# Preparation of a transformer block in another order: three table loads, x statistics block by block, and the later rotation tables made inside later groups

## What is computed

```
x = x + layernorm(attention(layernorm(x)))
x = x + layernorm(ffn(layernorm(x)))

# attention, per head h (64 complex dimensions)
q, k, v = complex projections of x
ang = t * [omega, -omega];  qr, kr = q*exp(i ang), k*exp(i ang)      # rotation tables: sin and cos of ang
E = exp(clip(-mu_h * |t - t'|, -30, 0))
s = Re(qr . conj(kr));  maha = max(|q|^2 + E^2 |k|^2 - 2 E s, 0) / V
logits = coef * log1p(maha / nu) - 32 * log(V);  A = causal softmax(logits);  y = A v
```

## Time and profile before

| what | us |
|---|---|
| runs | 1907.39, 1908.41, 1909.68 |
| median | 1908.41 |
| the profiled execution | 1907.7 |
| its span in the trace | 1905.9 |

### The profile page before, as it was taken

How to read it: one execution, slowest core, us unless ns; L and a number is a source line. 1 busy time by engine, 2 the same in 40 slices (tenths; PEclk the granted TensorE clock), 3 DMA queues, 4 the chain that set the end, 5 groups by cost and what they waited for, 6 DMA issues and landing times.

```text
span 1905.9 us, 40909 instructions
## 1 busy us (share of the span) xinstructions
PE 1798.5 (94%) x10672; PEld 1477.9 (78%) x10672; DVE 1609.2 (84%) x3842; ACT 1578.6 (83%) x3224; POOL 1453.4 (76%) x1288
## 2 busy tenths in 40 slices
PE   4589999999999999999999999999999999998997
PEld 3377788887888887887888778887888788876876
DVE  7788898888888887888888878888888888996884
ACT  5779888898888887888888888888888888886664
POOL 5367788888888887888888877888888888872663
PEclk8799999999999999999999999999999999999998
DMA  7313101231122111311013111211131111010111
GB/s 210 119 40 111 62 24 44 78 94 45 45 78 88 33 42 47 110 62 46 33 69 94 46 47 64 89 43 46 45 111 45 46 45 42 26 54 14 45 45 45
DMA packets 61087, 117.72 MB, mean 62 GB/s; under 512 B 13488, under 2 KB 42928, under 8 KB 52704
## 3 DMA queue, kind: packets, MB, share of 16 engines
q1 hardware_dynamic: 59936, 115.51, 18.0%
q10 hardware_dynamic: 960, 0.00, 0.0%
HBM read 99.64 MB, written 21.36 MB: 63 GB/s over the span
## 4 chain that ended last, share of the span: by engine, by line
PE 60%; DVE 10%; POOL 8%; issue 6%; ACT 2%; DVEq 0%; POOLq 0%; ACTq 0%
PE pa L786 13%; PE ps L826 11%; PE py L850 10%; PE po L861 9%; PE pp L816 7%; PE pp L838 5%; POOL qk L608 4%; PE pa L797 3%; PE pa L805 2%; DVE lg L1607 2%; DVE stats L1645 1%; POOL ek L618 1%; DVE ps L1596 1%; DVE lg L1615 1%; DVE acc L1667 1%
## 5 line engine op out<-in xcount | busy, mean ns | idle before, releaser
L608 POOL TENSOR_TENSOR qk<-rm 64x512 f32<-64x512 f32 x504 | 684.2, 1357 | 102.7 <-PE ps L826 44.2
L618 POOL TENSOR_TENSOR ek<-tabs,kn 128x512 f32<-128x512 f32 (+3 forms) x512 | 460.7, 906 | 151.7 <-DVE lg L1607 112.1
L1615 DVE CUSTOM_DVE_ANT_0 lg<-lg,tabs,ncog 128x512 f32<-128x512 f32 (+3 forms) x512 | 442.6, 883 | 0.6 <-issue 0.6
L786 PE MATMUL pa<-xt,wt 128*128 128x512 f32 x1488 | 424.4, 421 | 12.5 <-issue 6.9
L826 PE MATMUL ps<-qk 128*128 128x512 f32 (+3 forms) x1024 | 375.0, 450 | 25.0 <-DVE lg L1607 24.9
L1488 DVE TENSOR_TENSOR rm<-pa,tabs 128x512 f32<-128x512 f32 x504 | 327.9, 678 | 70.8 <-POOL qk L608 65.7
L1607 DVE CUSTOM_DVE_ANT_0 lg<-ps,ek,qb 128x512 f32<-128x512 f32 (+3 forms) x512 | 279.5, 546 | 125.3 <-POOL ek L618 82.7
L850 PE MATMUL py<-pt,vt 128*128 128x128 f32 x2560 | 347.9, 275 | 0.1
L850 PEld LDWEIGHTS py<-pt,vt 128*128 128x128 f32 x2560 | 330.6, 191 | 16.5 <-issue 0.3
L786 PEld LDWEIGHTS pa<-xt,wt 128*128 128x128 f32 x1488 | 275.9, 193 | 66.1 <-issue 11.2
L1186 ACT ACTIVATE lg<-lg,qb 128x512 f32<-128x512 f32 (+3 forms) x512 | 278.5, 558 | 19.4 <-DVE lg L1607 15.9
(11 more groups left out here) (193 smaller groups left out, 2245.2 us busy)
## 6 DMA issues: line engine op xcount, KB each, us to landing
xt<-xs_d SPq DMA_DIRECT2D x56, 1024.0 KB, 4.8
tabs<-vec_d SPq DMA_DIRECT2D x7, 1536.0 KB, 9.6
xs_d<-xt SPq DMA_DIRECT2D x6, 1024.0 KB, 4.0
wt<-wraw_d SPq DMA_DIRECT2D x7, 768.0 KB, 5.6
acc<-in_L_attn_x SPq DMA_DIRECT2D x8, 512.0 KB, 6.0
tabs<-in_L_attn_x SPq DMA_DIRECT2D x8, 512.0 KB, 4.9
out<-tabs SPq DMA_DIRECT2D x8, 512.0 KB, 3.1
tabs<-rope_d SPq DMA_DIRECT2D x56, 64.0 KB, 4.1
```

Of the source, the lines that this page charges most:

```text
L608: pool.tensor_tensor(qk[part * DH:(part + 1) * DH, z * HH + hh, :], rm[row, 2 * part, :], rm[row, 2 * part + 1, :], ALU.add if part else A ...
L618: pool.tensor_tensor(ek[:, n % 2, 0:w], tab(par, hh, E2_T, w), kn[:, hh, 0:w], ALU.mult).then_inc(ek_pool, 1)
L786: last = mm(pa[r][:, :], wproj(par, z, kt, a, r * P, (r + 1) * P), xbuf[x][:, kt, b, :], start=(n == 0), stop=(n == 3 * KT - 1))
L1615: dve.tensor_tensor_reduce(lg[:, hh, at(n)], lg[:, hh, at(n)], tab(par, hh, T3_T, w), ncog[:, par, 0, hh:hh + 1], 3e38, ALU.add, ALU.min, ...
```

## The change

1. ACT: the DMA of mu and its two activations come first, the sine table is loaded once, and all logarithms lie behind it: three table loads ahead of body 0 in place of five. The four omega DMAs move from ACT's queue to SP's.
2. x statistics go block by block; blocks 4 to 7 in bodies 0 to 3, behind `decay(c, 1, 3)`; before, two blocks each in bodies 0 and 1.
3. Of the feed-forward weights only one cast, two transposing steps and two keeps stay ahead of body 0; the rest are in body 0.
4. Body 0 makes only the first part of the rotation tables, with its five DVE instructions spread over the body, and ACT then waits for their store. Parts 1 to 3 are made in the free table tile `tabs[0]` in bodies 9, 10, 11 and 25, 26, 27 and 41, 42, 43: five angle instructions and a small copy on DVE over three bodies, and four activations on ACT in the third. The inner loop of those groups is written out for that.
5. Group 1's tables are loaded in body 5 (before 2 and 3), later groups' in their body 4 (before 2 and 3).

On ACT, ahead of body 0:

```diff
-            for k in range(ROPES):
-                act.dma_start(om[:, k:k + 1], omega_d[4 * k:4 * k + 4, :].rearrange("a (d e) -> (a d) e", e=1)).then_inc(om_all, 16)
...
+            act.wait_ge(mu_in, 16)
+            a_step(act.activation(hp[:, 6:7], hp[:, 0:1], ACT.Abs))
+            a_step(act.activation(hp[:, 11:12], hp[:, 6:7], ACT.Exp, scale=-1.0))
             first_high(0)
...
-            a_step(act.activation(hp[:, 16:21], hp[:, 11:16], ACT.Ln, bias=1.0))
             first_high(1)
...
             square(c0, 0, 0)
             square(c0, 0, 1)
-            ffn_cast_of(0)
+            a_step(act.activation(hp[:, 16:21], hp[:, 11:16], ACT.Ln, bias=1.0))
+            first_high(2)
+            x_normal(1)
...
             log(c0, 0, 1, 0)
-            ffn_cast_of(1)
-            ffn_cast_of(2)
+            ffn_cast_of(0)
+            ffn_keep(0)
             ffn_keep(1)
-            ffn_keep(2)
-            ffn_keep(3)
```

On ACT, in the body:

```diff
                 keep_values(c, it.slot, 1)
-                if it.own == 1:
-                    for k in range(ROPES):
-                        rope_trig(k)
-                    act.wait_ge(rope_act, 4 * ROPES + 3)
+                if it.rope == 0:
+                    rope_trig(first_rope, lambda n: 5 + n, lambda n: 3 + n)
+                    act.wait_ge(rope_out[0], 48)
+                if it.rope == 3:
+                    rope_trig(pair_rope, lambda n: act.snap(it.pair * 5 + (10 + n)), lambda n: act.snap(it.pair * 4 + (7 + n)))
                 log(c, 1, 3, it.slot)
                 keep_turned(c, 0, 0)
```

On DVE, in the body (`angle_turns`, `angle_whole`, `angle_first`, `angle_second` and `angle_clamp` are the five steps of one angle; the first two and the third of part 0 stand further ahead in body 0):

```diff
                 decay(c, 1, 2, it.par)
+                if it.rope == 0:
+                    angle_second(first_rope, first_angle)
+                    angle_clamp(first_rope, first_angle)
+                if it.rope == 1:
+                    pair_angles_ready(it.pair)
+                    angle_turns(pair_rope, pair_angle)
+                if it.rope == 2:
+                    angle_first(pair_rope, pair_angle)
+                if it.rope == 3:
+                    angle_clamp(pair_rope, pair_angle)
                 if nxt:
                     rotate(cn, it.behind, 1, RC)
...
-                if it.own == 1:
-                    all_angles_ready()
-                    for k in range(ROPES):
-                        rope_angle(k)
-                if it.own in (1, 2):
-                    x_stats(it.own + 2)
...
                 decay(c, 1, 3, it.par)
+                if it.own is not None and it.own < 5:
+                    x_stats(it.own + 3)
+                if it.rope == 1:
+                    angle_whole(pair_rope, pair_angle)
+                if it.rope == 2:
+                    angle_second(pair_rope, pair_angle)
                 distance(c, 1, 3, it.slot)
```

The bodies of each odd group:

```diff
-                with eng.Fori(0, B // 2 - 2) as i:
-                    inner(i, 1, None, 0)
-                    inner(i, 2, None, 0)
+                if par and not last:
+                    inner(0, 1, None, 0, 1)
+                    inner(0, 2, None, 0, 2)
+                    inner(1, 1, None, 0, 3)
+                    inner(1, 2, None, 0)
+                else:
+                    with eng.Fori(0, B // 2 - 2) as i:
+                        inner(i, 1, None, 0)
+                        inner(i, 2, None, 0)
```

More of the change, by code:

```diff
@@ L26 @@
 ACT = mybir.ActivationFunctionType
-It = namedtuple("It", "t half b par slot before behind b_before new opens raw part ready fresh own x xn over")
+It = namedtuple("It", "t half b par slot before behind b_before new opens raw part ready fresh own x xn over rope pair", defaults=(None, None))
+Rope = namedtuple("Rope", "turns ang sp sn om om2")
 B, N, D = 8, 512, 256
@@ L939, in body @@
                     project(cn, it.behind, 1 - it.slot, it.xn, half, it.own, 0, 1)
-                if it.own == 1:
-                    for n in range(6, 9):
-                        ffn_turn(n)
                 if old:
@@ L954, in body @@
                     project(cn, it.behind, 1 - it.slot, it.xn, half, it.own, 1, 0)
+                if it.own == 1:
+                    ffn_turn(3)
+                    ffn_turn(4)
+                    ffn_turn(5)
                 if old:
@@ L1294, in body @@
                     square(cn, 1, 0)
+                if it.own == 1:
+                    ffn_keep(3)
+                    ffn_keep(4)
+                    ffn_keep(5)
+                    ffn_cast_of(2)
                 if old:
@@ L1301, in body @@
                     square(cn, 1, 1)
+                if it.own == 1:
+                    ffn_keep(6)
+                    ffn_keep(7)
+                    ffn_keep(8)
                 log(c, 1, 1, it.slot)
@@ L1475, in x_low, with own_angle, first_angle @@
+            def own_angle(n):
+                return n
+            def first_angle(n):
+                return 5 + n
             def x_low(n, kt):
@@ L1714, in body, with pair_angle @@
                 old, nxt = it.before is not None, it.behind is not None
+                def pair_angle(n):
+                    return dve.snap(it.pair * 5 + (10 + n))
                 if it.opens is not None:
```

277 lines of the change are left out of this document (144 added, 133 removed).

## The result

| kernel | median of runs, us | runs | profiled execution | span | granted clock |
|---|---|---|---|---|---|
| before, beside the changed one | 1909.69 | 7, 1907.39 to 1911.52 | 1907.7 | 1905.9 | 0.982 |
| changed | 1917.2 | 7, 1910.78 to 1921.41 | 1910.78 | 1908.8 | 0.986 |

The ratio is 1.0037, with a 95% interval of 1.0025 to 1.005: slower, and outside the predicted range. The profiled execution of the changed kernel is the fastest of its seven; the others ran at a granted clock of 0.980 to 0.984 over the span. So two things have to be explained: 2.9 us between the two traces, and some 4.6 us more between the medians.

What follows compares the result with a forecast made beforehand. PE was taken to bound steady bodies, with DVE holding it up in body 0. Terms -3.7 - 7.4 - 1.7 + 10.2 = -2.6 us from 1907.7 gave 1905.1, stated as 1905.5; eight-in-ten range 1898.5 to 1912.

Steps and rivals of the forecast that it cites:

- What bounds the kernel: Steady body: PE busy all 25.10 us; ACT has 2.80 us and DVE 3.03 us of room, in small pieces.
- Preparation, -3.7: Ahead of body 0: PE's project of block 1 at 50.0 in place of 53.73; bounds 1 and 7 us.
- I let the two nearly cancel: Ahead of `ncog`: statistics and table loads saved against small steps beside POOL; first distance 0.55 us earlier.
- 1.47 + 1.1 + 0.6 = 3.2: Preparation behind the copy: one cast (1.47), two keeps (1.1) and one transposing step on PE (0.6) fewer.
- Body 0, -7.4: Body 0's stretch: 39.8 us in place of 47.2, DVE's block off the path, ACT late next; bounds 3.4 and 10.2.
- Statistics, -1.7: Three bodies beyond body 0: block-by-block statistics cost 3.0 us in place of 4.7; bounds a loss of 2, a gain of 4.
- Later tables, +10.2: Rotation tables in three later groups: 3.4 us per group, 2.7 for ACT and 0.7 for DVE; bounds 2.7 and 21.0.
- I take 2.7: ACT's sines ahead of `keep_turned(c, 0, 0)`: PE stands 2.5 us at its third transposition; cost taken as 2.7 per group.
- Writing out the inner loop costs nothing: Inner loop of the groups making later tables: no cost, since bodies 0 to 8 are written out too.
- dear tables: Rival: each later group pays ACT's and DVE's time in full, both delaying the loop through POOL; +8.2, 1915.9 us; chance 0.09.
- turning point of 5.5 us per group: Later tables: cost per group from which the dear-tables rival decides, (12.8 + 3.8) / 3.
- The stall only changes its engine: Rival: in body 0 ACT is late nearly as long as DVE was; gain 3.4 there; +4.1, 1911.8 us; chance 0.13.

Runs made afterwards that it cites:

- its repetition: The changed kernel run again as it is: 1917.21 us beside 1909.01, ratio 1.0051.
- the small steps first: The changed kernel with DVE's `x_move(1)` moved behind the 14 small steps on the 16-row vectors: 1915.49 us beside 1908.28, ratio 1.0039.
- the kernel before with sines: Kernel before, odd groups' bodies written out, plus a table load and four activations on idle data in bodies 11, 27, 43: 1921.5 us beside 1908.28, ratio 1.0062.

## Why the prediction was wrong, point by point

**What bounds the kernel.** Right. PE has no room in a steady body, and whatever stops it there is paid in full.

**Preparation, -3.7: measured -0.6.** The step "I let the two nearly cancel" (small steps against statistics) failed: the copy `ncog` came at 41.86, 2.7 us later than before, where 38.6 had been assumed. That is 3.2 us, and the small steps beside POOL, drawn out by 3.9 us, are what stands in DVE's full queue there; that they alone make up the 3.2 is argued and not shown, since the trial that moved them moved the shift as well. Behind it the chain did shorten by casts and keeps: from the copy to PE's project it takes 11.2 us, before 14.5, so 3.3 us, where the text counted 1.47 + 1.1 + 0.6 = 3.2. The term that was mis-sized is the one ahead of the copy:

```profile
42.04 1.26 ACT L1193 ACTIVATE kn<-pa,ncog 128x512 f32<-128x512 f32 x2 [4.57 <-DVE ncog L1850]
```

ACT waits 4.57 us for it here; before, the same activation began at 39.38.

**Body 0, -7.4: measured -8.8.** Right in mechanism: DVE's hole became one of ACT's, and PE stood 5.25 us ended by ACT (forecast some 5), at a clock of 0.96 in the second part (before 0.63). From the last activation's end (85.66) to the release at 89.21 the store took 3.5 us, as forecast (3.4); but the sum set the logarithm's table load of 1.28 us behind the wait, and it ran inside it, so that ACT idled only 2.25 us. Most of the 1.4 us above the forecast are this load:

```profile
85.68 1.28 ACT L1204 ACT_TABLE_LOAD   x1
89.21 0.40 ACT L1204 ACTIVATE lg<-lg,qb 128x128 f32<-128x128 f32 x1 [2.25 <-DMA rope_d<-pt]
...
90.24 0.66 PE L853 MATMUL pp<-ident,pr 128*128 128x128 f32 x2 [5.25 <-ACT pt L1219]
...
91.48 0.59 ACT L1187 ACTIVATE sq<-pa 128x512 f32<-128x512 f32 x1
```

**Statistics, -1.7: measured -1.4.** Right: bodies 1 to 4 are 28.36 to 28.38 apart, 0.9 more than 27.43. One premise was partly luck: the 4.7 us that two-block statistics cost before hold a fall of the clock (0.95 over that interval, behind a stand of PE of 3.15 us), which the text didn't read.

**Later tables, +10.2: measured +13.8 in the trace, and about 15 where all three stands lower the clock.** This is the step that decided. The stand was sized at 2.5 and the interval's growth at 2.7, and 2.55 and 2.8 were measured. What failed is "I take 2.7": the sum ended with the stand. PE comes out of it at the lower clock in most cases (2 of 3 in the profiled execution, 3 of 3 in its repetition, 2 of 3 with the small steps first, 3 of 3 in the kernel before with sines), and pays 1.2 to 1.4 us more in the changed kernel and its repetition, 1.3 and 2.1 with the small steps first, and 2.1 to 2.3 (against the 27.9 of the changed kernel) where the sines stood in the kernel before. Of the 3.6 us missed in the trace 2.7 are the clock. The prediction had the granted clock of body 0 before its eyes and priced no fall here. DVE's part was 1.4 in group 1 in place of 0.7, inside the bounds of 0 to 3.3. With PE kept busy over the stand the median came to 1910.89: this one term decides between inside and outside the range.

The page "ScalarE: Activation LUTs" of the Trainium skill, in "What ACT_TABLE_LOAD costs", adds a drain of 1.38 us to every switch. The changed kernel's rows at 381.38 and 385.27 settle it for this kernel: the loads take 1.28 us, each starts within 0.05 us of the end of the activation ahead of it, and there is no drain. So the loads are not what was underpriced.

**"Writing out the inner loop costs nothing".** Right as it stands for the kernel before, where it even gave 5 us, for a reason that isn't shown. For the changed kernel it was incomplete: intervals 23, 39 and 55 grew by 0.65 us each, of which 0.31 are seen at DVE's `logits`, lasting 1.23 us beside POOL in place of 0.92. Such differences of phase came and went with the edits here, between 0 and 6.8 us over the kernel.

**The rivals.** The one on the other side with dear tables (1915.9) gives nearly the measured time, but by luck: its mechanism, both engines' work paid in full, isn't what happened. Per group 4.2 us are paid of 7, plus the clock. Its turning point of 5.5 us per group was about reached (4.2, and 5.4 to 5.6 with the clock). "The stall only changes its engine" fell.

**The median.** The forecast took the profiled execution as typical, with a median 0.7 us above it (which makes 1905.8; it said 1905.5). For the changed kernel it lies 6.4 us under the median of its runs, and at a clock of 0.986 against 0.980. In the trace of the repetition (span 1913.3, so 4.4 us longer) intervals 1, 25 and 44 are longer by 1.2, 1.6 and 1.4 and the feed-forward tail by 2.3, each at a lower clock; interval 41 is shorter by 1.2 at a higher one, and the mark of body 0 comes 0.9 earlier. The kernels in which the sines' stand is broken up or filled run at 0.987 and 0.986 in the median, the changed one at 0.981. So between these two traces the gap is how often the clock falls; that it is so for the slower runs, of which no trace was kept, is argued and not shown.

## What to carry to other kernels

Where PE is the bound and its stream is dense, price a stop of PE as the stop and the slow matmuls behind it (here 2.8 us and 1.2 to 2.3 more), and look for an order in which the same wait comes in pieces or with work in it. Move side work to where PE waits anyway, not to where the engine that does it has its average room. Before trusting a sum of few microseconds, set the profiled execution beside the spread of the runs: with the added stands of PE the seven runs spread over 10.6 us, where the kernel before has 4.1 beside them.

## What the runs showed of the hardware

- A stand of 2.55 to 2.60 us in a steady body came with a stretch at the lower clock in 10 of 12 cases (six matmuls in 2.45 to 2.91 us in place of 1.63); stands of up to 1.32 us at the same place never did, in 6 of 6. More work on PE made the kernel 6.3 us faster. The length of the stand alone doesn't decide: stands of 3.39 and 3.38 us in body 0 of two kernels, and 7 of the 28 at the back edge (below), left the clock at 1.00.
- A VectorE `logits` instruction of the same shape took 0.73, 0.92, 1.23 or 1.46 us (the first and last at one place of the program, the middle two at another), as POOL's instruction had 0.12, 0.37, 0.69 or 0.91 us to go when it began: the remainder and some 0.55 to 0.6. From before, body 23:

```profile
679.43 1.28 POOL L608 TENSOR_TENSOR qk<-rm 64x512 f32<-64x512 f32 x1 [0.23 <-DVE rm L1488]
680.34 0.92 DVE L1615 CUSTOM_DVE_ANT_0 lg<-lg,tabs,ncog 128x512 f32<-128x512 f32 x1
```

and from the changed kernel:

```profile
674.50 1.30 POOL L622 TENSOR_TENSOR qk<-rm 64x512 f32<-64x512 f32 x1 [0.53 <-DVE rm L1513]
675.11 1.23 DVE L1645 CUSTOM_DVE_ANT_0 lg<-lg,tabs,ncog 128x512 f32<-128x512 f32 x1
```

- At the outer loop's back edge PE waits 2.81 to 3.69 us with nothing to wait for in the profile ("issue"), and the clock fell in 21 of 28 cases; the interval varied from 28.3 to 31.9 us between the traces, and by 1.6 and 1.2 us between two executions of the same kernel.
